# Score products on half the contraction rows and four heads each, in one score tile across two PSUM banks

## The chip, the cores and the metric

The kernel runs on one NeuronCore of a Trainium2 chip. The metric is the device time of one execution in microseconds (us); lower is better. Engines are named as in the profile: PE (TensorE, the matrix products; PEld is its weight load), DVE (VectorE), ACT (ScalarE), POOL (GpSimd) and SP (SyncE, which here issues the transfers).

## The reference, cut to what matters

The input x is 128 sequences of 32 tokens with 256 features. In the first layer each sequence is mixed along its 32 tokens by a 32 x 32 matrix that its subject picks, then goes through an attention whose four projections have quantised inputs and weights, and is added to x. A second mixing and a mixture of 16 experts (2 per token) follow. The change lies in the score products of the attention:

```
q, k, v = bitlinear(x, wq), bitlinear(x, wk), bitlinear(x, wv)   # each (128, 32, 256) -> 16 heads of 16
attn = einsum('bhqd,bhkd->bhqk', q, k) / sqrt(16)                # 16 heads, 32 x 32 scores per sequence
attn = where(causal, attn, -inf); attn = softmax(attn, -1)
out = einsum('bhqk,bhkd->bhqd', attn, v)
x = x + bitlinear(out, wp)
x = x + moe(mix(x))
```

## The kernel before

**Tiling.** The 4096 tokens are 32 tiles of 128 (`TILES`), four sequences each (`BT`), and a group is four tiles (`TG`, `GROUPS` = 8). Features live in two chunks of 128 (`KC` = 2), so a chunk holds 8 heads of 16 rows (`HC` = 8).

**The scores as block products.** Heads must not mix, though a product contracts over all its 128 rows. So the keys are spread out: `kx[g % 2]` has, for each chunk and each of its 8 heads, a copy of the transposed keys in which only the 16 rows of that head are filled, and the rest is zero for good (ACT clears `kx[0]` at L546, POOL clears `kx[1]` in `zero_kx1`, L464). `spread_k` (SP, L344) fills them with 8 transfers of 64 KB per group, once DVE has scaled the keys into `kT` (`scale_k`, L857). One product of `scores` (PE, L1180) then takes the 32 queries of one sequence as weights, 128 rows by 32 columns, and streams 8 heads times 32 keys, 256 columns; four sequences fill the four quarters of the output partitions. Two chunks and four sequences make 8 products of fp32 per tile, all on top of one product that lays down the causal mask (L1176, 512 columns, bf16). The result, 128 x 512, is one PSUM bank; tiles alternate between two banks, `ps_s[t % 2]`.

**What follows a score tile.** `copy_scores` (ACT, L636) copies the bank to `sc[t % 2]`, `row_max` (DVE, L867) takes the maximum per head, `sub_max` (POOL, L482) subtracts it, `exp_` (ACT, L647) takes the exponential, `transpose_p` (PE, L1193) and `copy_pT` (ACT, L658) turn it round, and `attend` (PE, L1208) multiplies by the values.

**The order of the work.** Each engine has one instruction stream, written out by hand in a function `iteration(it)` that is unrolled for `it` = 0 to 11. It works on several groups at once: mixing and projecting group `it`, scores and softmax of group `it - 1`, output projection of group `it - 2` (with its own quantisation: `centre_o` L573, `largest_o` L832, `factor_o` L838, `round_o` L582, `transpose_o` L1114, `project_o` L1219), second mixing, router (L1257) and ranks of group `it - 3`, and the scattering of rows to the experts' lists (POOL, L492) for group `it - 4`. Engines wait for each other by counting semaphores; a buffer is free when the count of its reader has come. For a score tile PE waits until ACT has copied the tile before the last (`sc_copied`).

After the loop 79 tiles of 128 rows pass the experts (L1335 to L1353 on PE), and the results are gathered and added up (L1059, L1061). This part uses the same memory (`arena`) for its weights, and starts to load them after the last score products that read it.

## Time and profile before

| | |
|---|---|
| median of 3 runs | 433.49 us (433.41 to 436.78) |
| profiled execution | 433.42 us, of it the span of the trace 431.6 us |
| PE busy | 324.8 us (75%) |
| DVE busy | 263.8 us (61%) |
| ACT busy | 248.7 us (58%) |
| POOL busy | 213.2 us (49%) |
| score products (L1180) | 35.8 us, in 512 records |
| mask products (L1176) | 12.6 us, in 32 records |

The span falls into a start of about 28 us, the loop over groups to about 252 us, the experts to about 400 us, and the gathering. Busy times are unions, so products that run side by side count once. A share of the whole span says little here: what an edit in the loop is worth is read from the loop.

### The profile page before, as it was taken

To read this page: it belongs to the slowest core of one execution; us is meant where nothing else is said; L and a number is where in the kernel's file an instruction comes from. 1 tells how busy PE (TensorE), PEld (TensorE's weight loads), DVE (VectorE), ACT (ScalarE), POOL (GpSimd) and SP (SyncE) were. 2 spreads that over 40 slices of the span, in tenths; PEclk is the share of its full clock that TensorE was granted. 3 is DMA by queue.
4 is the path that set the end of the run, shared out by engine and by line. 5 is a ranking of instruction groups with operands and counts; after the bars stand their busy time and mean duration, and the time that the engine had idled before them with its cause. 6 is when DMAs were issued, how large, how long until landed. Compare 5 with 4: busy or idle time off the path is not lost.

```text
span 431.6 us, 10950 instructions
## 1 busy us (share of the span) xinstructions
PE 324.8 (75%) x3257; PEld 249.9 (58%) x3257; DVE 263.8 (61%) x929; ACT 248.7 (58%) x580; POOL 213.2 (49%) x232
## 2 busy tenths in 40 slices
PE   0535989999999999999985800999799979993000
PEld 0332455767676676767574700898689868992000
DVE  2544477898888989898785373344344433441775
ACT  9144468787796978788676220566466645662000
POOL 3643123122473755647577854276657664664000
PEclk9968799999999999999997655899999999998555
DMA  6613555544546362534566695566646654631999
GB/s 232 173 53 68 137 114 114 116 102 82 124 134 161 99 182 66 159 85 119 145 186 185 165 293 205 141 180 170 176 133 179 177 159 120 183 100 32 379 400 357
DMA packets 76897, 68.87 MB, mean 160 GB/s; under 512 B 41003, under 2 KB 65968, under 8 KB 76721
## 3 DMA queue, kind: packets, MB, share of 16 engines
q1 hardware_dynamic: 65200, 44.03, 40.7%
q0 software_dynamic: 7296, 20.02, 12.7%
q10 hardware_dynamic: 4352, 4.20, 2.8%
q8 instruction: 28, 0.46, 0.5%
q14 instruction: 21, 0.16, 0.1%
HBM read 35.36 MB, written 30.62 MB: 153 GB/s over the span
## 4 chain that ended last, share of the span: by engine, by line
PE 46%; DVE 14%; issue 12%; DMA 6%; POOL 6%; SPq 6%; DVEq 5%; ACT 3%; POOLq 1%; ACTq 0%
PE bank L1342 9%; PE bank L1353 6%; PE bank L1180 5%; SPq L413 4%; POOL y_d L537 4%; DMA arena<-y_d 3%; PE bank L1335 3%; PE bank L1231 3%; PE bank L1257 3%; PE bank L1129 2%; SPq L344 2%; PE bank L1114 2%; PE bank L1208 2%; PE bank L1244 2%; PE bank L1193 2%
## 5 line engine op out<-in xcount | busy, mean ns | idle before, releaser
L537 POOL DMA_INDIRECT y_d<-cen,di x79 | 77.4, 980 | 53.2 <-issue 32.1
L1044 DVE SCALAR_TENSOR_TENSOR kT<-kT,hrow,bank 128x96 f32<-128x96 f32 x79 | 24.8, 314 | 78.4 <-ACT kT L732 77.6
L492 POOL DMA_INDIRECT routed<-hrow,posi x64 | 63.2, 987 | 17.0 <-issue 15.4
L1342 PE MATMUL bank<-arena,qT 128*128 x316 | 66.5, 334 | 0.0
L482 POOL TENSOR_TENSOR sc<-sc,mx 128x512 f32<-128x512 f32 x32 | 33.5, 1048 | 65.8 <-DVE mx L867 65.7
L1342 PEld LDWEIGHTS bank<-arena,qT 128*128 128x128 f32 x316 | 51.2, 196 | 0.2
L1335 PE MATMUL bank<-ident,hrow 128*128 128x128 f32 x158 | 31.7, 282 | 25.1 <-DMA hrow<-routed 19.0
L1353 PE MATMUL bank<-arena,sc 96*128 x158 | 48.0, 386 | 0.0
L737 ACT ACTIVATE cen<-bank 128x256 f32<-128x256 f32 x79 | 30.4, 384 | 25.0 <-PE bank L1353 24.0
L727 ACT ACTIVATE qT<-bank 128x256 f32<-128x256 f32 x79 | 29.9, 379 | 25.7 <-PE bank L1335 25.5
L1335 PEld LDWEIGHTS bank<-ident,hrow 128*128 128x128 f32 x158 | 22.5, 146 | 34.1 <-DMA hrow<-routed 19.7
L1180 PE MATMUL bank<-arena,qT 128*32 128x256 f32 x512 | 35.8, 399 | 0.0
L732 ACT ACTIVATE kT<-bank 128x96 f32<-128x96 f32 x79 | 19.9, 251 | 18.1 <-PE bank L1342 16.5
L658 ACT ACTIVATE pT<-bank 128x512 f32<-128x512 f32 x32 | 19.7, 614 | 12.2 <-PE bank L1193 11.8
L636 ACT ACTIVATE sc<-bank 128x512 f32<-128x512 f32 x32 | 19.6, 612 | 11.8 <-PE bank L1180 11.8
L1353 PEld LDWEIGHTS bank<-arena,sc 96*128 96x128 f32 x158 | 24.1, 192 | 3.6 <-issue 0.5
L867 DVE TENSOR_REDUCE mx<-sc 128x16 f32<-128x512 f32 x32 | 21.8, 680 | 4.9 <-ACT sc L636 4.9
L647 ACT ACTIVATE pr<-sc,s_qk 128x512 f32<-128x512 f32 x32 | 23.5, 735 | 2.0 <-POOL sc L482 1.8
L1208 PE MATMUL bank<-vx,pT 128*32 128x68 f32 x1024 | 21.8, 224 | 2.4 <-DVE cen L878 1.2
L1208 PEld LDWEIGHTS bank<-vx,pT 128*32 128x32 f32 x1024 | 16.8, 108 | 11.0 <-issue 6.6
L1180 PEld LDWEIGHTS bank<-arena,qT 128*32 128x32 f32 x512 | 13.7, 112 | 16.2 <-issue 11.0
L667 ACT ACTIVATE hrow<-bank 128x512 f32<-128x512 f32 x32 | 17.5, 603 | 9.2 <-PE bank L1231 7.7
(169 smaller groups left out, 732.1 us busy)
## 6 DMA issues: line engine op xcount, KB each, us to landing
hrow<-routed SPq DMA_DIRECT2D x79, 129.0 KB, 2.5
arena<-y_d SPq DMA_DIRECT2D x16, 512.0 KB, 12.3
v_d<-v_sb SPq DMA_DIRECT2D x8, 544.0 KB, 4.0
vx<-v_d SPq DMA_DIRECT2D x32, 136.0 KB, 3.5
X<-in_x SPq DMA_DIRECT2D x8, 512.0 KB, 3.7
arena<-kT SPq DMA_DIRECT2D x64, 64.0 KB
out_x<-X ACTq DMA_DIRECT2D x16, 256.0 KB, 8.7
arena<-in_L_ffn_gate_w SPq DMA_DIRECT2D x4, 384.0 KB, 3.6
```

Source lines behind the costliest of these rows:

```text
L482: g_.tensor_tensor(sc[t % 2][:, :, :], sc[t % 2][:, :, :], mx[t % 2][:, :].unsqueeze(2).to_broadcast([P, H, SEQ]), ALU.subtract).then_inc( ...
L492: g_.indirect_dma_start(routed, bass.IndirectOffsetOnAxis(ap=posi[g % 2][:, t, k:k + 1], axis=0), hrow[:, g % 2, t, k, :], None).then_inc( ...
L537: g_.indirect_dma_start(y_d, bass.IndirectOffsetOnAxis(ap=di[:, n:n + 1], axis=0), ye[n], None, bounds_check=Y_ROWS - 1, oob_is_err=False) ...
L647: a_.activation(pr[t % 2][:, :, :, :].rearrange("p c s j -> p s c j"), sc[t % 2][:, :, :].rearrange("p (s c) j -> p s c j", c=SLOTS), ACT. ...
L727: a_.activation(xeT[j % 2], bank[j % 2][:, 0:D].rearrange("p (c t) -> p c t", c=KC), ACT.Copy).then_inc(xeT_copied, 1)
L737: a_.activation(ye[n], bank[6 + n % 2][:, 0:D], ACT.Copy).then_inc(ye_copied, 1)
L1044: v.scalar_tensor_tensor(out=hh[n % 2], in0=sg[n % 2], scalar=xe[n][:, D + 1:D + 2], in1=bank[2 + n % 2][:, F:2 * F], op0=ALU.mult, op1=AL ...
L1180: last = t_.matmul(ps_s[t % 2][b * SEQ:(b + 1) * SEQ, c * HC * SEQ:(c + 1) * HC * SEQ], qT[g % 2][:, c, cols], kx[g % 2][:, c, :, cols], s ...
L1208: last = t_.matmul(o[b * SEQ:(b + 1) * SEQ, :, c, :], pT[t % 2][:, c, b * SEQ:(b + 1) * SEQ], vx[:, t * BT + b, :, c * VW:(c + 1) * VW], s ...
L1335: last = t_.transpose(bank[j % 2][:, c * P:(c + 1) * P], xe[j][:, c * P:(c + 1) * P], ident[:, :])
L1342: last = t_.matmul(bank[2 + n][:, 0:2 * F], xeT[n][:, c, :], gu[:, c, bass.ds(expert[m + LAG - 1], 1), :].rearrange("p o f -> p (o f)"), s ...
L1353: t_.matmul(bank[6 + n][:, 0:D], hhT[n], dw[:, bass.ds(expert[m], 1), :].rearrange("p o d -> p (o d)"), start=True, stop=True).then_inc(ye ...
```

## The change

It touches five places.

- The key buffers hold four heads per chunk side by side instead of eight (`HR` = 4): head h of a chunk lies in its 16 rows, at slot `h % 4`. Rows 0 to 63 of a slot so hold heads 0 to 3, and rows 64 to 127 heads 4 to 7. Each buffer is half as long, and so is its clear.
- A score product takes 64 rows (one half, `r`) instead of 128 and streams 4 heads, 128 columns, instead of 256. There are 16 per tile instead of 8, and the mask product becomes two of 256 columns.
- The two row halves write to two banks, `pair[:, 0]` and `pair[:, 1]`, each half filled. Both banks together are one tile; there is no second. So PE waits for the copy of the tile just before (`t` instead of `t - 1` in the count of `sc_copied`).
- The copy reads both half banks in one instruction and puts the heads back in their order in `sc`.
- In the order of the work, PE computes tile 2 after the two transposes of x instead of before them, and ACT copies tile 1 before `centre_o` and tile 2 before `copy_v(it, 0)`.

```diff
+HR = HC // 2
+HALF = KC * HR * SEQ
...
-    KX_WORDS = KC * HC * GT
-
-    kx = [arena[:, i * KX_WORDS:(i + 1) * KX_WORDS].rearrange("p (c h t) -> p c h t", c=KC, h=HC) for i in range(2)]
+    KX_WORDS = KC * HR * GT
+
+    kx = [arena[:, 2 * i * KX_WORDS:(2 * i + 1) * KX_WORDS].rearrange("p (c h t) -> p c h t", c=KC, h=HR) for i in range(2)]
...
-    bank = [ctx.enter_context(nc.psum_tensor(f"bank{i}", [P, 512], fp32)) for i in range(8)]
+    bank = [ctx.enter_context(nc.psum_tensor(f"bank{i}", [P, 512], fp32)) for i in range(3)]
+    pair = ctx.enter_context(nc.psum_tensor("pair", [P, 2, 512], fp32))
+    bank += [pair[:, 0, :], pair[:, 1, :]]
+    bank += [ctx.enter_context(nc.psum_tensor(f"bank{i}", [P, 512], fp32)) for i in range(5, 8)]
...
-                    sp.dma_start(kx[g % 2][rows, :, h, :], kT[rows, :, :]).then_inc(kx_in, 16)
+                    sp.dma_start(kx[g % 2][rows, :, h % HR, :], kT[rows, :, :]).then_inc(kx_in, 16)
...
-                a_.activation(sc[t % 2][:, :, :].rearrange("p h j -> p (h j)"), ps_s[t % 2][:, :], ACT.Copy).then_inc(sc_copied, 1)
+                a_.activation(sc[t % 2][:, :, :].rearrange("p (c r k) j -> p r c (k j)", c=KC, r=2),
+                              pair[:, :, 0:HALF].rearrange("p r (c n) -> p r c n", c=KC), ACT.Copy).then_inc(sc_copied, 1)
...
                 copy_scores(it - 1, 0)
+                copy_scores(it - 1, 1)
                 centre_o(it - 2)
-                copy_scores(it - 1, 1)
...
+                copy_scores(it - 1, 2)
                 copy_v(it, 0)
-                copy_scores(it - 1, 2)
...
-                if t >= 2:
-                    wait(pe, sc_copied, g, TG, t - 1)
+                if t >= 1:
+                    wait(pe, sc_copied, g, TG, t)
                 else:
-                    wait(pe, sc_copied, g, TG, TG + t - 1, lag=1)
-                t_.matmul(ps_s[t % 2][:, :], ident_b[:, :], causal_b[:, :].unsqueeze(1).to_broadcast([P, H, SEQ]), start=True, stop=False, skip_group_check=True)
+                    wait(pe, sc_copied, g, TG, TG, lag=1)
+                for r in range(2):
+                    t_.matmul(ps_s[r][:, 0:HALF], ident_b[:, :], causal_b[:, :].unsqueeze(1).to_broadcast([P, H // 2, SEQ]), start=True, stop=False, skip_group_check=True)
                 for c in range(KC):
                     for b in range(BT):
                         cols = slice(t * P + b * SEQ, t * P + (b + 1) * SEQ)
-                        last = t_.matmul(ps_s[t % 2][b * SEQ:(b + 1) * SEQ, c * HC * SEQ:(c + 1) * HC * SEQ], qT[g % 2][:, c, cols], kx[g % 2][:, c, :, cols],
-                                         start=False, stop=True, skip_group_check=True)
+                        for r in range(2):
+                            rows = slice(r * P // 2, (r + 1) * P // 2)
+                            last = t_.matmul(ps_s[r][b * SEQ:(b + 1) * SEQ, c * HR * SEQ:(c + 1) * HR * SEQ], qT[g % 2][rows, c, cols], kx[g % 2][rows, c, :, cols],
+                                             start=False, stop=True, skip_group_check=True)
...
                 mix2(it - 3, 1)
-                scores(it - 1, 2)
                 transpose_x(it, 0)
                 transpose_x(it, 1)
+                scores(it - 1, 2)
                 spread_s(it)
```

On PE, the stretch of a full turn from score tile 0 on stands so before (L1176 and L1180 are a score tile, L1257 the router, L1231 the second mixing, L1100 the transposes of x):

```order
L1176 MATMUL bank<-causal_b,ident_b 128x512 [waits sc_copied,q_copied,kx_in]
L1180 MATMUL bank<-arena,qT 32x256 x8
L1257 MATMUL bank<-rw,hT 128x16 [waits hT_copied,rw_in]
L1257 MATMUL bank<-rw,hT 128x16 x7
L1176 MATMUL bank<-causal_b,ident_b 128x512 [waits sc_copied]
L1180 MATMUL bank<-arena,qT 32x256 x8
L1231 MATMUL bank<-X,bd_0 128x256 [waits h_copied]
L1231 MATMUL bank<-X,bd_0 128x256
L1176 MATMUL bank<-causal_b,ident_b 128x512 [waits sc_copied]
L1180 MATMUL bank<-arena,qT 32x256 x8
L1100 MATMUL bank<-ident,cen 128x128 [waits z1_ok]
L1100 MATMUL bank<-ident,cen 128x128 x3
```

and after the change, from the router on, with L1183 and L1189 the score tile, L1266 the router, L1240 the mixing and L1106 the transposes:

```order
L1266 MATMUL bank<-rw,hT 128x16 [waits hT_copied,rw_in]
L1266 MATMUL bank<-rw,hT 128x16 x7
L1183 MATMUL pair<-causal_b,ident_b 128x256 [waits sc_copied]
L1183 MATMUL pair<-causal_b,ident_b 128x256
L1189 MATMUL pair<-arena,qT 32x128 x16
L1240 MATMUL bank<-X,bd_0 128x256 [waits h_copied]
L1240 MATMUL bank<-X,bd_0 128x256
L1106 MATMUL bank<-ident,cen 128x128 [waits z1_ok]
L1106 MATMUL bank<-ident,cen 128x128 x3
L1106 MATMUL bank<-ident,cen 128x128 [waits z1_ok]
L1106 MATMUL bank<-ident,cen 128x128 x3
L1183 MATMUL pair<-causal_b,ident_b 128x256 [waits sc_copied]
```

A tile is now two masks and 16 products on half as many columns, and tile 2 has moved behind the transposes.

On ACT, the stretch from the copy of tile 0 to that of V stands so before (L636 is the copy, L573 the centring of O, L667 the rows for the experts, L591 the copies of the transposes of x, L625 the copy of V):

```order
L636 ACTIVATE sc<-bank 128x512 [waits exp_ok,sc_ready]
L573 ACTIVATE cen<-cen,nmean 128x256 [waits o_var_ok]
L573 ACTIVATE cen<-cen,nmean 128x256 x3
L636 ACTIVATE sc<-bank 128x512 [waits exp_ok,sc_ready]
L667 ACTIVATE hrow<-bank 128x2x256 [waits h_ready]
L667 ACTIVATE hrow<-bank 128x2x256
L591 ACTIVATE xq<-bank 128x512 [waits v_ready,q_ready,xqT_ready] x2
L647 ACTIVATE pr<-sc,s_qk 128x4x4x32 [waits pT_ready,s1_ok,sub_ok]
L605 ACTIVATE s_row<-bank 128x512 [waits k_scaled,srow_ready]
L681 ACTIVATE ratio<-second 128x4 [waits second_ok]
L625 ACTIVATE v_sb<-bank,s_v 128x16x16 [waits v_put,s1_ok,v_ready]
L625 ACTIVATE v_sb<-bank,s_v 128x16x16
```

and after the change (L641, L578, L673, L596 and L630 in the same roles):

```order
L641 ACTIVATE sc<-pair 128x2x2x128 [waits exp_ok,sc_ready] x2
L578 ACTIVATE cen<-cen,nmean 128x256 [waits o_var_ok]
L578 ACTIVATE cen<-cen,nmean 128x256 x3
L673 ACTIVATE hrow<-bank 128x2x256 [waits h_ready]
L673 ACTIVATE hrow<-bank 128x2x256
L596 ACTIVATE xq<-bank 128x512 [waits v_ready,q_ready,xqT_ready] x2
L653 ACTIVATE pr<-sc,s_qk 128x4x4x32 [waits pT_ready,s1_ok,sub_ok]
L610 ACTIVATE s_row<-bank 128x512 [waits k_scaled,srow_ready]
L687 ACTIVATE ratio<-second 128x4 [waits second_ok]
L641 ACTIVATE sc<-pair 128x2x2x128 [waits exp_ok,sc_ready]
L630 ACTIVATE v_sb<-bank,s_v 128x16x16 [waits v_put,s1_ok,v_ready]
```

The copies of tiles 0 and 1 now stand together ahead of the centring, and that of tile 2 ahead of V.

## Rows read from the trace of the kernel before

**Rows 1.** Timeline of PE: start us, length us, operation, count [idle before <-releaser].

```profile
157.05 0.68 PE L1208 MATMUL bank<-vx,pT 128*32 128x68 f32 x32 [0.20 <-DVE cen L878]
...
181.45 0.68 PE L1208 MATMUL bank<-vx,pT 128*32 128x68 f32 x32 [0.21 <-DVE cen L878]
```

**Rows 2.** Busy us of PE, PEld, DVE, ACT, POOL in one turn; clock; DMA.

```profile
157.60:182.00 24.40, 24.09 (x327) 17.24 (x316) 21.96 (x79) 19.82 (x42) 14.14 (x14) 1.00 0.46 120
```

**Rows 3.** All waits of DVE from 84 to 206 us: total, times, longest.

```profile
DVE rs L876 <- PE bank L1208: 0.5, 1, 0.5
DVE amax L804 <- issue: 0.4, 1, 0.4
```

**Rows 4.** Timeline of DVE, then of POOL, in that turn.

```profile
162.49 1.14 DVE L825 TENSOR_SCALAR cen<-cen,mul 128x256 f32<-128x256 f32 x4
...
168.49 1.07 DVE L838 TENSOR_SCALAR amax<-amax 128x4 f32<-128x4 f32 x1
...
169.75 0.69 DVE L857 TENSOR_TENSOR kT<-bank,s_row 128x512 f32<-128x512 f32 x1
...
168.48 1.04 POOL L482 TENSOR_TENSOR sc<-sc,mx 128x512 f32<-128x512 f32 x1 [0.89 <-DVE mx L867]
```

**Rows 5.** Groups: shape, count | busy us, mean ns | idle before <-releaser.

```profile
L1180 PE MATMUL bank<-arena,qT 128*32 128x256 f32 x512 | 35.8, 399 | 0.0
...
L1208 PE MATMUL bank<-vx,pT 128*32 128x68 f32 x1024 | 21.8, 224 | 2.4 <-DVE cen L878 1.2 <-ACT pT L658 0.7
...
L636 ACT ACTIVATE sc<-bank 128x512 f32<-128x512 f32 x32 | 19.6, 612 | 11.8 <-PE bank L1180 11.8
...
L1176 PE MATMUL bank<-causal_b,ident_b 128*128 128x512 bf16 x32 | 12.6, 394 | 5.9 <-DMA arena<-kT 5.9
```

**Rows 6.** Timeline of PE, same turn: score tile 0, then the router.

```profile
158.94 1.07 PE L1180 MATMUL bank<-arena,qT 128*32 128x256 f32 x16
159.94 1.96 PE L1257 MATMUL bank<-rw,hT 128*128 128x16 f32 x16
```

**Rows 7.** Timeline of ACT, same turn: copy of tile 0, centring, copies of x.

```profile
160.13 0.63 ACT L636 ACTIVATE sc<-bank 128x512 f32<-128x512 f32 x1
160.60 1.74 ACT L573 ACTIVATE cen<-cen,nmean 128x256 f32<-128x256 f32 x4
...
166.03 1.08 ACT L591 ACTIVATE xq<-bank 128x512 bf16<-128x512 f32 x2 [0.72 <-PE bank L1100]
```

**Rows 8.** Timeline of PE: transposes of group 0, first mask and score tile.

```profile
28.48 1.97 PE L1100 MATMUL bank<-ident,cen 128*128 128x128 f32 x8 [7.01 <-DVE cen L825]
...
43.24 0.61 PE L1176 MATMUL bank<-causal_b,ident_b 128*128 128x512 bf16 x1 [4.37 <-DMA arena<-kT]
43.78 1.94 PE L1180 MATMUL bank<-arena,qT 128*32 128x256 f32 x16
```

**Rows 9.** Timeline of PE: transposes in the second turn with scores.

```profile
67.97 1.09 PE L1100 MATMUL bank<-ident,cen 128*128 128x128 f32 x8 [0.64 <-DVE cen L825]
```

**Rows 10.** Timelines of ACT and DVE, last turn with scores.

```profile
208.72 1.69 ACT L573 ACTIVATE cen<-cen,nmean 128x256 f32<-128x256 f32 x4
...
211.95 1.21 DVE L832 TENSOR_REDUCE amax<-cen 128x4 f32<-128x1024 f32 x1
...
213.85 1.06 DVE L838 TENSOR_SCALAR amax<-amax 128x4 f32<-128x4 f32 x1
```

**Rows 11.** Groups: the two clears of the key buffers.

```profile
L546 ACT ACTIVATE arena<-arena 128x8192 uint32<-128x8192 uint32 x1 | 7.0, 7030 | 0.0
L464 POOL MEMSET arena<- 128x8192 f32 x1 | 6.9, 6919 | 4.0 <-DVE cen L825 4.0
```

**Rows 12.** Busy us of the engines and granted clock in three stretches.

```profile
43.24:47.60 4.36, 4.36 (x34) 1.39 (x34) 3.09 (x11) 0.60 (x1) 0.42 (x1) 0.50 0.51 132
...
228.60:231.90 3.30, 1.28 (x12) 0.76 (x11) 2.98 (x17) 2.14 (x6) 2.49 (x4) 1.00 0.38 96
...
309.10:312.40 3.30, 0.13 (x1) 0.16 (x2) 0.38 (x3) 0.38 (x1) 1.78 (x2) 1.00 0.62 174
```

## The prediction

> **What bounds the kernel now.** I read the page first (it says PE 75%, DVE 61%, ACT 58% of the span), and then looked at where the changed work lies: the score products run only in the loop over groups, from 43 us on [rows 8]. What lies after that (routing, the 79 expert tiles, the last sums) keeps its instructions, so only the loop can move the time. The second view is the timeline of one full turn. Its first and last rows [rows 1] are the same 32 products, 24.40 us apart: this is the period of the loop, and before each of them PE has waited 0.2 us for a VectorE result. The busy time of that turn [rows 2] looks as if PE were the bound (24.09 of 24.40) and DVE had 2.4 us to spare (21.96). The third view corrects this. In the five turns from 84 to 206 us DVE waited for anybody just twice, 0.9 us in all [rows 3]. Its spare 2.4 us are the pauses of 0.07 to 0.10 us that its drains leave between small operations, some 28 in a turn: it is in its own order, back to back. A part of its turn is neither work nor a wait that a view names: an operation on 4 columns (L838) stands with 1.07 us, just as long as POOL's subtraction beside it [rows 4]; DVE released that subtraction itself, with the row maximum before it. So **two engines are full**, DVE with nothing spare and PE with 0.2 us. Time taken from PE alone buys nothing in a full turn.
>
> **The products.** Each fp32 product stands in the trace as two records: 16 for the 8 products of a score tile (rows 5 count 512 for 32 tiles), 32 for the 16 of the attention. The 16 records of a score tile take 1.07 us with the tail of the last, 1.00 until PE goes on [rows 6]; their mean of 399 ns each, 16 in 1.07 us, shows several running at once, on the four output quarters. After the change it has 32 records on half the columns. Bounds: if the two row halves run side by side, half the columns give 0.50; if they don't, it stays 1.00. The row nearest to the new shape is L1208, also 32 records, of 68 columns and 32 output rows: 21.8/32 = 0.68 us per tile, 21 ns per record [rows 5]. I take 0.62 us, between 0.50 and 0.68: **0.38 us saved per tile**, 1.5 per full turn. Far out stands the case that each record keeps its 62 ns: 2.0 us. The Trainium skill (TensorE: Matmul & The Clock Gate, section Back-to-back issue gap) has a floor of about 25 ns from start to start however few columns there are. By that floor 32 records take 0.80 us and a tile saves 0.20. The trace does not agree (21 ns in L1208), so the row decides.
>
> The mask product becomes two of 256 columns instead of one of 512 (12.6/32 = 0.39 with its tail, 0.22 before the next starts): same columns, one more weight load, which overlaps. I charge 0 to 0.1 us and take 0.05.
>
> **The single tile.** Scores of tile t now wait for the copy of tile t-1 instead of t-2. The copy is 0.61 us [rows 5], and with the handing over on both sides it is 0.7 from the last product to the next. In a full turn, in the clock times of rows 6 and 7:
> - Tile 0 to 1: the router stands between, 1.9 us [rows 6]. Tile 0 ends at 159.6, its copy cannot start before ACT is free (160.13 [rows 7]), and is over at 160.8; the router ends at 161.5. Wait 0.
> - Tile 1 to 2: mix2 and the transposes stand between. These wait for DVE (L825 ends at 163.63 [rows 4]), as PE comes to them at 163.4 (tile 1 to 162.35, mix2 1.06): wait 0.2. Tile 2 then stands behind the transposes, while ACT copies them out (1.1 us [rows 7]), time in which PE did the spreading of the scales before.
> - Tile 2 to 3: its copy was moved ahead of the V copy on ACT, and lands at 168.4; PE arrives at 168.1. Wait 0.3.
> - On ACT, the centring of O (L573, 1.74 us) is queued behind copy 1, so behind tile 1: it ends at 164.5 instead of 162.3. DVE comes to it 1.9 us before its L838, that is at 166.6 (the maximum over O, 1.21, and a row maximum, 0.68, lie between), so it costs nothing here.
> - After tile 3 PE needs DVE's scaled keys (L857, 170.44 [rows 4]); it was there at 170.5 before and is there early now, and waits.
>
> So PE saves 1.5, gives 0.5 back in new waits and idles for the rest. What DVE takes from PE and ACT (the four copies, router scores, ranks, projections) arrives 0.2 us or more earlier or at the time before. **Full turns: 0.** No transfer changes its size; the key DMAs are released by DVE's L857, thus at the same times.
>
> **The first turns.** Scores of group 0 start at 43.24, when the keys land, at half clock: 1.9 us a tile [rows 8]. Tile 0 and 1 save 0.9 each, the copy between them costs 0.7, the transposes come 1.1 earlier and so partly into half clock, which costs 0.5, and tiles 2 and 3 save 0.7. With 0.2 lost in meeting ACT, this is **1.1 less**. In the next turn PE was idle before the transposes, with tile 2 done [rows 9]. Now tile 2 stands behind them, on the path: +0.9, of which tile 3 gives back 0.38 and ACT's queue hides 0.1: **+0.4**.
>
> **The last turn with scores** (207 us on) has no transposes of x and DVE is not full. There the centring counts: it ran at 208.72, while ACT waited for tile 1 [rows 10]. Now: tile 0 ends at 207.75, router to 209.65, tile 1 to 210.6, copy to 211.2, centring (1.7) to 212.9. DVE's L832 started on it at 211.95 and now can at 212.9; L838 behind it (again beside POOL) gives ACT its factors 0.9 later, and the transposes of O, project_o and the residual follow. **+0.9.** If DVE's other operations (den, pos) took its place, it would be +0.5.
>
> **Zeroing** kx halves from 7.0 (ACT) and 6.9 us (POOL) [rows 11]. ACT's is its first work, long before DVE's first moments let it go on; POOL's starts with the end of DVE's first L825, at 28.4, and only the second group's keys need it, a turn later. Nothing waits for either: 0. If DVE was slowed by it, it would be a gain of some tenths.
>
> **The clock.** PE's gaps grow from 0.64 to 1.9 us in the second turn with scores, and one of 0.7 is put into the first burst, which ran without a gap at half clock (1.2 GHz) for 4.4 us before 2.4 GHz was granted [rows 12]. Around 228.6 a stretch with 1.28 us busy of 3.30 was followed by half clock, yet a pause of 3.2 us among the expert tiles was not [rows 12]. So a lost stretch is possible at three places (43, 66 and 212 us). The eight transposes take 1.97 us at half clock [rows 8] and 1.09 at full [rows 9], so what PE has to do there, some 1.6 us of it on the path each time, costs as much again: 0 to 1.6 us per place. I take 0.8 for the three together.
>
> **Sum:** -1.1 + 0.4 + 0 + 0.9 + 0.8 = +1.0, against the profiled execution of 433.42 us (span 431.6), which stands 0.07 below the median of the runs, 433.49. Forecast **434.4 us**.
>
> **Rivals.**
> 1. **The row halves don't overlap** (they do leave through separate banks, but nothing in this trace shows two row halves at once). Then PE keeps its 24.1 us of work and gets 0.5 us of waits and 0.2 of masks: 24.8 to 25.0 per turn instead of 24.4. PE becomes the bound: 0.5 over six turns (the five full ones and the one before) is +3.0, and the first turns lose their gain (+1.1): 438.5. It decides as soon as a tile takes over 0.9 us. For it: no row here. Chance 0.10.
> 2. **The copy becomes the bound.** If ACT is late at each tile, PE stands 0.7 us four times, 2.8 against 1.5 saved. A turn is 24.1 + 1.3 = 25.4, six turns +6.0: 440. It decides once ACT begins a copy later than the work between two tiles lasts. Against it: the router and the transposes between the tiles [rows 6]. Chance 0.05. The Trainium skill (TensorEngine Tiling (Array Packing), section PSUM Bottleneck) points this way: tiling speeds up the products but not their way out of PSUM.
> 3. **PE was the bound** and DVE only looks full, because its pauses and the 1.07 us rows stretch. Then 1.5 - 0.5 = 1.0 per turn comes back, six turns -6, the ends +0.2: 428. Against it: rows 3 and the 0.2 us that PE waits for DVE each turn. Chance 0.07.
> 4. **Records keep their pace** of 62 ns: 1.0 more per tile, over 20 us slower. Chance 0.03.
>
> The forecast has the remaining 0.75. It includes up to three clock stretches (to 438) and none of them (433.6), and the ends of the ramps (431.9 if the last turn costs nothing and the clock holds). The **range** is 431.6 to 438.6: it leaves out rivals 2, 3 and 4 and little else. A change of 1%, 4.3 us, is about what a measurement of this kernel can tell from none. Faster by more: rival 3, 0.07. Slower by more: rivals 1, 2 and 4, 0.18. Within: 0.75.
>
> **What would show it.** In the changed profile: the group of score products at 0.6 us per tile with 32 records; PE's idle time before the transposes and before tile 3's mask, released by DVE and by the ACT copy; the period between two turns still 24.4, with DVE's list of waits as short as before; DVE's L832 of the last turn late; the granted clock at 44 to 50, 66 to 72 and 212 to 218. The prediction is wrong if the period of the full turns moves by over 0.3 us either way, or if DVE in them waits for PE or ACT.

## The result, and the profile after

| | before | after |
|---|---|---|
| median | 433.86 us (432.02 to 436.78, 20 runs) | 436.55 us (434.97 to 440.12, 20 runs) |
| ratio after/before | | 1.0064, 95% interval 1.0045 to 1.0083 |
| profiled execution (span) | 433.42 (431.6) | 437.44 (435.7) |

The changed kernel is 2.7 us slower, 0.6%. Another series, that of e4 below, gave 438.00 against 434.47 (ratio 1.0085, 1.0053 to 1.0118). Ratios leave out executions over 1.5% above the fastest of their kernel: one of twelve in e2 and in e3, and five of twelve in e6, its profiled one among them. The length of the changed kernel's profile and the busy times of its page:

```profile
span 435.7 us, 12023 instructions
...
PE 313.3 (72%) x3786; PEld 254.0 (58%) x3801; DVE 263.7 (61%) x929; ACT 244.5 (56%) x580; POOL 209.6 (48%) x232
```

PE has 11.5 us less to do, DVE what it had, ACT and POOL 4.2 and 3.6 less (most of it the halved clears), and the kernel is slower. The groups that answer to [rows 5] and [rows 11] (shape, count | busy, mean ns | idle before):

```profile
L1189 PE MATMUL pair<-arena,qT 64*32 64x128 f32 x1024 | 22.2, 284 | 0.0
L641 ACT ACTIVATE sc<-pair 128x512 f32<-128x512 f32 x32 | 19.5, 608 | 17.0 <-PE pair L1189 17.0
L1183 PE MATMUL pair<-causal_b,ident_b 128*128 128x256 bf16 x64 | 12.9, 284 | 7.2 <-DMA arena<-kT 5.7 <-ACT sc L641 1.5
L551 ACT ACTIVATE arena<-arena 128x4096 uint32<-128x4096 uint32 x1 | 3.6, 3616 | 0.0
L469 POOL MEMSET arena<- 128x4096 f32 x1 | 3.5, 3507 | 4.0 <-DVE cen L831 4.0
```

The product group fell from 35.8 to 22.2 us, the two clears halved, the masks and copies stand as they were. Now the full turn of [rows 1], [rows 2], [rows 4] and [rows 6], first PE's timeline (start, length, operation, count [idle before <-releaser]):

```profile
157.81 0.68 PE L1217 MATMUL bank<-vx,pT 128*32 128x68 f32 x32 [0.21 <-DVE cen L884]
...
159.38 0.38 PE L1183 MATMUL pair<-causal_b,ident_b 128*128 128x256 bf16 x2
159.69 0.67 PE L1189 MATMUL pair<-arena,qT 64*32 64x128 f32 x32
160.29 1.96 PE L1266 MATMUL bank<-rw,hT 128*128 128x16 f32 x16
...
164.44 1.09 PE L1106 MATMUL bank<-ident,cen 128*128 128x128 f32 x8 [0.31 <-DVE cen L831]
...
171.58 0.38 PE L1135 MATMUL bank<-xq,wT 128*128 128x512 bf16 x1 [1.01 <-DVE kT L863]
...
182.22 0.68 PE L1217 MATMUL bank<-vx,pT 128*32 128x68 f32 x32 [0.21 <-DVE cen L884]
```

A score tile lasts 0.60 us until PE goes on (159.69 to 160.29). No wait for the copy L641 stands in the turn; PE waits for DVE instead, 1.01 us at the scaled keys, and the period is 24.41. That turn in the view of busy time (length, then busy us of PE, PEld, DVE, ACT, POOL, granted clock, DMA share, GB/s), and all waits of DVE from 84 to 206 us:

```profile
157.60:182.00 24.40, 22.59 (x382) 17.48 (x384) 21.96 (x78) 19.69 (x42) 14.13 (x14) 1.00 0.45 116
```

```profile
DVE mv L791 <- issue: 0.5, 1, 0.5
DVE amax L810 <- issue: 0.4, 1, 0.4
```

PE gave up 1.50 us of the turn, DVE's 21.96 us are those of [rows 2], and its waits sum to the same 0.9 us as in [rows 3]. So the full turns are as forecast, and the time was lost elsewhere. The four turns between the first masks of groups 2 to 6 last 24.36, 24.45, 24.76, 24.40 before and 24.35, 24.47, 24.76, 24.42 after.

**The ends of the loop.** The second turn with scores, PE:

```profile
63.35 0.39 PE L1183 MATMUL pair<-causal_b,ident_b 128*128 128x256 bf16 x2 [1.04 <-DMA arena<-kT]
63.67 0.67 PE L1189 MATMUL pair<-arena,qT 64*32 64x128 f32 x32
65.10 0.39 PE L1183 MATMUL pair<-causal_b,ident_b 128*128 128x256 bf16 x2 [0.76 <-ACT sc L641]
...
68.00 1.09 PE L1106 MATMUL bank<-ident,cen 128*128 128x128 f32 x8 [1.91 <-DVE cen L831]
68.92 0.38 PE L1183 MATMUL pair<-causal_b,ident_b 128*128 128x256 bf16 x2
69.24 0.67 PE L1189 MATMUL pair<-arena,qT 64*32 64x128 f32 x32
69.83 1.16 PE L1130 MATMUL bank<-ident,step_of 128*128 128x128 f32 x8
```

The transposes come when DVE lets them, at 68.00 as at 67.97 in [rows 9]; PE's idle time before them grew from 0.64 to 1.91 us, and tile 2 stands behind them. The turn lasts 22.45 us instead of 21.76. The last turn with scores, DVE, ACT and PE, for [rows 10]:

```profile
211.27 1.69 ACT L578 ACTIVATE cen<-cen,nmean 128x256 f32<-128x256 f32 x4
...
213.00 1.22 DVE L838 TENSOR_REDUCE amax<-cen 128x4 f32<-128x1024 f32 x1 [1.16 <-ACT cen L578]
...
214.90 1.06 DVE L844 TENSOR_SCALAR amax<-amax 128x4 f32<-128x4 f32 x1
...
219.85 1.05 PE L1228 MATMUL bank<-wT,oq 128*128 128x256 bf16 x8 [0.30 <-ACT oq L603]
```

DVE now waits 1.16 us for O's centring. Counted from the first mask of the last group (206.76 before, 206.97 after), project_o starts 12.88 us later instead of 12.11.

**This pair of profiles does not show the loss.** On the clock of the execution project_o was 0.97 us late (219.85 against 218.88), yet the experts began at the same time. The last half of the last group's second mixing ran at half clock in the profile before and at full clock in the one after, and that alone gave 0.94 us back. Before, then after:

```profile
245.99 2.05 PE L1231 MATMUL bank<-X,bd 128*128 128x256 f32 x4
...
268.74 1.51 PE L1335 MATMUL bank<-ident,hrow 128*128 128x128 f32 x4 [19.03 <-DMA hrow<-routed]
```

```profile
246.97 1.11 PE L1240 MATMUL bank<-X,bd 128*128 128x256 f32 x4
...
268.73 1.33 PE L1344 MATMUL bank<-ident,hrow 128*128 128x128 f32 x4 [19.03 <-DMA hrow<-routed]
```

The 4.1 us between the two spans lie behind that, 2.0 in the experts and 2.1 in what follows them, where no instruction changed and where profiles of one kernel differ by as much. The loss shows in the medians; what it is made of has to be read from the turns of many profiles.

### The profile page after: what moved, and what is told of

Its sections match the earlier page's. It is cut to its first block, busy times and chain, and to the rows that moved or that the text cites. A ratio compares the mean times of both kernels' runs of the same rounds, so it can differ in the third digit from the quotient of the medians.

```text
span 435.7 us, 12023 instructions
## 1 busy us (share of the span) xinstructions
PE 313.3 (72%) x3786; PEld 254.0 (58%) x3801; DVE 263.7 (61%) x929; ACT 244.5 (56%) x580; POOL 209.6 (48%) x232
## 4 chain that ended last, share of the span: by engine, by line
PE 37%; DVE 22%; issue 13%; DVEq 7%; POOL 6%; DMA 6%; SPq 5%; ACT 3%; POOLq 1%; ACTq 0%
PE bank L1362 6%; PE pair L1351 5%; PE bank L1351 5%; SPq L418 4%; POOL y_d L542 4%; PE bank L1344 3%; DMA arena<-y_d 3%; DVE stats L891 2%; PE bank L1120 2%; DVE X L901 2%; PE bank L1253 2%; DVE cen L884 2%; DVE stats L785 2%; PE bank L1228 2%; PE bank L1135 2%
## 5 line engine op out<-in xcount | busy, mean ns | idle before, releaser
L487 POOL TENSOR_TENSOR sc<-sc,mx 128x512 f32<-128x512 f32 x32 | 33.5, 1047 | 66.7 <-DVE mx L873 66.6
L1050 DVE SCALAR_TENSOR_TENSOR kT<-kT,hrow,bank 128x96 f32<-128x96 f32 x40 | 12.6, 315 | 39.9 <-ACT kT L738 39.1
L1050 DVE SCALAR_TENSOR_TENSOR kT<-kT,hrow,pair 128x96 f32<-128x96 f32 x39 | 12.3, 314 | 40.4 <-ACT kT L738 40.4
L1351 PE MATMUL bank<-arena,qT 128*128 x160 | 34.0, 337 | 0.0
L1351 PE MATMUL pair<-arena,qT 128*128 x156 | 33.8, 342 | 0.0
L641 ACT ACTIVATE sc<-pair 128x512 f32<-128x512 f32 x32 | 19.5, 608 | 17.0 <-PE pair L1189 17.0
L1351 PEld LDWEIGHTS bank<-arena,qT 128*128 128x128 f32 x160 | 26.3, 198 | 0.4 <-issue 0.3
L1351 PEld LDWEIGHTS pair<-arena,qT 128*128 128x128 f32 x156 | 26.1, 201 | 0.0
L569 ACT ACTIVATE cen<-bank,nmean 128x256 f32<-128x256 f32 x32 | 12.5, 475 | 19.7 <-DVE veps L794 19.7
L475 POOL TENSOR_TENSOR rstd<-veps,half 128x4 f32<-128x4 f32 x8 | 8.2, 1029 | 31.8 <-DVE veps L794 31.8
```

Source lines behind the costliest of these rows:

```text
L487: g_.tensor_tensor(sc[t % 2][:, :, :], sc[t % 2][:, :, :], mx[t % 2][:, :].unsqueeze(2).to_broadcast([P, H, SEQ]), ALU.subtract).then_inc( ...
L1050: v.scalar_tensor_tensor(out=hh[n % 2], in0=sg[n % 2], scalar=xe[n][:, D + 1:D + 2], in1=bank[2 + n % 2][:, F:2 * F], op0=ALU.mult, op1=AL ...
L1351: last = t_.matmul(bank[2 + n][:, 0:2 * F], xeT[n][:, c, :], gu[:, c, bass.ds(expert[m + LAG - 1], 1), :].rearrange("p o f -> p (o f)"), s ...
```

## The experiments

They ran in three series, each on a chip of its own and each against the kernel before on that chip: e1 to e4, e5 to e8, and e9 to e11. Only the first of the three has the changed kernel in it (e4), so across series ratios are compared and not times. Theories: A, the new order costs time at the loop's ends. B, the single score tile makes PE or ACT wait in every turn. C, later stages shift by chance. D, shorter products leave gaps in which TensorE's granted clock stays at or falls to 1.2 GHz.

**e1, old order on half rows.** Single tile and half rows stay; PE and ACT get their old order (B, or the shape alone, against A).

```diff
-                transpose_x(it, 0)
-                transpose_x(it, 1)
                 scores(it - 1, 2)
+                transpose_x(it, 0)
+                transpose_x(it, 1)
...
                 copy_scores(it - 1, 0)
-                copy_scores(it - 1, 1)
                 centre_o(it - 2)
+                copy_scores(it - 1, 1)
...
-                copy_scores(it - 1, 2)
                 copy_v(it, 0)
+                copy_scores(it - 1, 2)
```

> The changed kernel with the order of before: PE computes tile 2 ahead of the transposes of x, ACT centres O between the copies of tiles 0 and 1 and copies V before tile 2. The half-row products and the single tile stay. Theory A (the loss comes from the new order: tile 2 behind the transposes in the second turn with scores, +0.4 to +0.7, and the centring behind tile 1 in the last, +0.3 to +0.9): 1 to 1.6 us faster than the changed kernel, so a ratio to before of about 1.001 or less, and in its profile the centring of O in the last turn starts right behind the copy of tile 0. Theory B (the loss comes from the single tile, whose wait the order was meant to hide): slower than the changed kernel, 438 or more, with full turns over 24.4 us. Theory C (the loss lies outside the loop, in the clock of the later stages): no difference beyond 0.5 us.

Measured: 436.73 us, ratio 1.0053 (1.0024 to 1.0082). Full turns 24.19 to 24.76 us, so the single tile costs nothing there and B falls for the full turns. In the first turn, where tile 2 now stands right behind tile 1, it does cost time: PE waits 0.76 us for the copy ahead of tile 1 and again ahead of tile 2, and the turn takes 20.89 us instead of 19.70. The last group's project_o came 11.68 us after its first mask, so the order is what had cost time there. Yet theory A's ratio of 1.001 or less did not come: the second turn with scores lasted 24.05 us, with the clock fallen. That started theory D.

**e2, new order alone.** The kernel before (full rows, two tiles) in the new order.

```diff
-                scores(it - 1, 2)
                 transpose_x(it, 0)
                 transpose_x(it, 1)
+                scores(it - 1, 2)
...
                 copy_scores(it - 1, 0)
-                centre_o(it - 2)
                 copy_scores(it - 1, 1)
+                centre_o(it - 2)
...
-                copy_v(it, 0)
                 copy_scores(it - 1, 2)
+                copy_v(it, 0)
```

> The kernel before with the new order alone (PE's tile 2 behind the transposes, ACT's copies of tiles 1 and 2 earlier); full-row products, two tiles. Theory A: the order costs its 1 to 1.5 us here too, and more where PE is full: PE has only 0.2 us to spare per turn, and tile 2 now stands in front of the spreading of the scales, so up to 0.3 us per turn: ratio to before 1.003 to 1.007. Theory B: no difference. Theory C: no difference, or one as large as in the changed kernel if it comes from the order through the clock.

Measured: 437.82 us, ratio 1.0072 (1.0035 to 1.0109). The order alone makes this kernel as slow, as theory A forecast (up to 1.007), and without the clock: its mean time at half clock is 94.9 us per execution, where the kernel before has 92.7 in that series. Second turn 23.02 us (at 2.4 GHz throughout), project_o of the last turn 13.63 us after the first mask, 1.5 later than before: full tiles make the centring wait longer than half ones.

**e3, PE's old order only.** The changed kernel; ACT keeps the new order.

```diff
-                transpose_x(it, 0)
-                transpose_x(it, 1)
                 scores(it - 1, 2)
+                transpose_x(it, 0)
+                transpose_x(it, 1)
```

> The changed kernel with only PE's order put back (tile 2 ahead of the transposes); ACT keeps the new order. Theory A: the second turn with scores gets its 0.4 to 0.9 us back, the last turn does not: 0.5 to 0.9 faster than the changed kernel and slower than with both put back by 0.3 to 0.9. Theory B: PE waits for the copy of tile 1 before tile 2 in every turn, 0.2 to 0.7 us, hidden or not; if not hidden, full turns of 24.6 to 25.1. Theory C: no difference.

Measured: 438.61 us, ratio 1.0085 (1.0054 to 1.0116), level with the changed kernel (e4) and not 0.5 to 0.9 faster as theory A had it. The last turn is as in the changed kernel (12.87), so that loss comes with ACT's order and not PE's. The first turn with scores is 21.66 us, 2 more than in the changed kernel; the second 23.67, with the clock down in it.

**e4, the changed kernel again**, word for word, as control in the same series.

> The changed kernel once more, word for word, for a second profile and its time against before on this chip. Ratio 1.0045 to 1.0083 as measured. Theory A and B: the loop from the landing of the first keys to the last score tile takes the same as in its first profile, within 0.3 us. Theory C: the later stages (experts, gathering) differ from profile to profile by 1 to 3 us with the position of the half-clock stretches, and the mean of them is what the change costs.

Measured: 438.00 us, ratio 1.0085. Its profile differs from the first one of the same kernel in one place, the second turn with scores, PE:

```profile
64.33 0.67 PE L1189 MATMUL pair<-arena,qT 64*32 64x128 f32 x32
67.83 1.97 PE L1106 MATMUL bank<-ident,cen 128*128 128x128 f32 x8 [2.83 <-DVE cen L831]
69.59 0.63 PE L1183 MATMUL pair<-causal_b,ident_b 128*128 128x256 bf16 x2
70.15 1.05 PE L1189 MATMUL pair<-arena,qT 64*32 64x128 f32 x32
```

After 2.83 us without work the eight transposes take 1.97 us instead of 1.09 and the tile 1.05 instead of 0.67: the clock is at half. This turn took 24.84 us instead of 22.45, 0.9 of it from the first mask to the transposes, and 1.5 behind them. The 0.9 began a turn earlier: the first burst of the scores ran at half clock for 7.9 us instead of 6.0, and DVE released the transposes 25.15 us after the first mask of all instead of 24.35.

**e5, the gaps of the second turn filled.** Products without a use, from the identity and the projection weights, into a bank that is free then.

```diff
+            def fill(n, ps):
+                for _ in range(n):
+                    t_.matmul(ps[:, :], ident_b[:, :], wT[:, 0, :, :].rearrange("p c o -> p (c o)"), start=True, stop=True)
...
+                if it == 2:
+                    fill(4, ps_c)
                 scores(it - 1, 0)
                 router(it - 3)
+                if it == 2:
+                    fill(3, ps_c)
                 scores(it - 1, 1)
                 mix2(it - 3, 1)
+                if it == 2:
+                    fill(8, ps_c)
```

> The changed kernel with 15 additional products on TensorE (identity by 512 columns of the projection weights, 0.21 us each at 2.4 GHz, into the router's bank, which nothing uses yet), all in the second turn with scores: 4 ahead of the first score tile (TensorE idles 1.04 us there), 3 ahead of the second (0.76), 8 ahead of the transposes of x (1.91). They leave the result alone and keep TensorE at work where it otherwise waits. Theory D (clock): the changed kernel's shorter products leave gaps in this turn, and in many executions the granted clock falls to 1.2 GHz there; that turn lasted 22.45 us where it stayed and 24.84 where it fell. With the gaps filled the clock stays in every execution: second turn 22.3 to 22.6 us in the profile, mean time per execution at half clock about 97 us instead of 102 to 107, median lower by 1 to 1.5 us, ratio to the kernel before about 1.005. Theory A (order of the work alone): a turn's length does not hang on what fills TensorE's waits; nothing changes, ratio 1.0085 as in the control run of the changed kernel.

Measured: 436.34 us, ratio 1.0037 (1.0010 to 1.0063). The kernel does more work and its ratio is lower than the changed kernel's in either series, though the intervals overlap. PE in that turn:

```profile
66.19 0.67 PE L1189 MATMUL pair<-arena,qT 64*32 64x128 f32 x32
66.80 1.90 PE L1287 MATMUL bank<-wT,ident_b 128*128 128x512 bf16 x8
68.87 1.09 PE L1106 MATMUL bank<-ident,cen 128*128 128x128 f32 x8 [0.17 <-DVE cen L831]
```

The turn is 22.55 us, the transposes run at full clock. The mean time per execution at half clock (worked out as twice the missing part of the mean granted clock times the span) was 95.7 us, against 106.6 in e4 and 102.3 in the first series of the changed kernel.

**e6, O's centring put back in the last turn alone.**

```diff
                 copy_scores(it - 1, 0)
+                if it == GROUPS:
+                    centre_o(it - 2)
                 copy_scores(it - 1, 1)
-                centre_o(it - 2)
+                if it != GROUPS:
+                    centre_o(it - 2)
```

> The changed kernel, where in the last turn with scores alone (it == GROUPS) ScalarE centres O between the copies of tiles 0 and 1, as before the change, and in every other turn behind the copy of tile 1. Theory A (order): the last turn loses the 1.0 us that O's maximum came late (14.. the turn from first mask to last mask of the last group 8.3 to 7.3 us), everything behind it follows 1.0 us earlier, median 1.0 us under that of the changed kernel, ratio to the kernel before 1.0085 - 0.0023 = about 1.006. Theory D (clock alone): the 1.0 us comes back at the last turn but the stage of the experts takes it up, since TensorE's clock there depends on when the pause begins; ratio 1.0085.

Measured: 435.58 us over all 12 executions against 434.12, that is 1.0034; the ratio 0.9998 (0.9960 to 1.0035) rests on seven of them, so I build on neither. The trace of the last turn shows what the edit did there, DVE:

```profile
214.33 1.21 DVE L841 TENSOR_REDUCE amax<-cen 128x4 f32<-128x1024 f32 x1
216.22 1.07 DVE L847 TENSOR_SCALAR amax<-amax 128x4 f32<-128x4 f32 x1
```

Its first mask is at 209.54, so the maximum starts 4.79 us later; in the changed kernel it was 6.03 (213.00 - 206.97). Project_o follows at 11.63 instead of 12.88. This profile had half clock in the second turn again, which took 25.83 us.

**e7, every loss mended.** e6, tile 2 ahead of the transposes in the second turn, and products without a use in three places.

```diff
+                if it == 1:
+                    fill(8, ps_c)
+                if it == 2:
+                    fill(4, ps_c)
                 scores(it - 1, 0)
                 router(it - 3)
+                if it == 2:
+                    fill(3, ps_c)
                 scores(it - 1, 1)
                 mix2(it - 3, 1)
+                if it == 2:
+                    fill(3, ps_c)
+                if it == 2:
+                    scores(it - 1, 2)
+                    fill(3, ps_c)
                 transpose_x(it, 0)
                 transpose_x(it, 1)
-                scores(it - 1, 2)
+                if it != 2:
+                    scores(it - 1, 2)
...
                 iteration(it)
+            fill(70, ps_c)
```

> The changed kernel with the place of each loss mended: ScalarE's old order in the last turn, TensorE's old place of tile 2 (ahead of the transposes of x) in the second turn with scores, and additional products without a use (8 ahead of the first score tile of all, 13 in the second turn with scores, 70 between the last ranking and the experts, where TensorE waits 19 us for the routed rows). Theory D with A: first turn 19.6 (new order) or less, second turn 22 or less without half clock, last turn 7.3, the stage of the experts begins at full clock and is 2 to 3 us shorter; median 431 to 433, ratio 0.992 to 0.998. If only the order counts: ratio 1.004, that is 436. If the additional products stand in the way of the work (they can't be overtaken), it is above the changed kernel's 1.0085.

Measured: 433.30 us, ratio 0.9974 (0.9946 to 1.0001). The loss is gone. The stage of the experts was not 2 to 3 us shorter: 125.86 us, where the kernel before has 125.75 to 128.91 (below).

**e8, the kernel before, filled.** Full rows, two tiles, old order, products without a use alone.

```diff
+                if it == 1:
+                    fill(8, ps_c)
+                if it == 2:
+                    fill(4, ps_c)
                 scores(it - 1, 0)
...
                 scores(it - 1, 2)
+                if it == 2:
+                    fill(3, ps_c)
...
+            fill(70, ps_c)
```

> The kernel before, with full rows, two score tiles and its own order, and additional products without a use: 8 ahead of the first score tile, 4 ahead of the second turn's first, 3 behind its third, 70 ahead of the experts. It tells what the two ways of making the score products are worth where the clock is the same in both. Theory D: both gain by the filled pause ahead of the experts; this one has 0.4 us more of score products in each tile, which costs nothing where VectorE sets the turn (24.4 us), and so it ends within 1 us of the kernel with half rows and filled gaps: median 431 to 433, ratio 0.993 to 0.998. Rival (score products on half the rows are worth something once the clock is out of the way): this one ends 1 to 3 us behind the other.

Measured: 432.47 us, ratio 0.9978 (0.9946 to 1.0010). e7 and e8 can't be told apart, nor either from no gain over the kernel before. With the losses at the ends mended, half rows are worth nothing that shows.

**e9, both causes mended, nothing else.** e5 and e6 together.

```diff
+                if it == 2:
+                    fill(4, ps_c)
...
+                if it == 2:
+                    fill(3, ps_c)
...
+                if it == 2:
+                    fill(8, ps_c)
...
+                if it == GROUPS:
+                    centre_o(it - 2)
                 copy_scores(it - 1, 1)
-                centre_o(it - 2)
+                if it != GROUPS:
+                    centre_o(it - 2)
```

> The changed kernel with the 15 additional products in the second turn with scores and, in the last turn alone, ScalarE's centring of O back between the copies of tiles 0 and 1. If the two causes add up (theory A for the last turn, 1.0 us; theory D for the second turn, 1.3 to 1.8 us), the last group's masks span 7.3 us, the second turn lasts 22.3 to 22.6 without half clock, and the kernel is level with the one before: ratio 0.999 to 1.003. If one of them only hid the other, it stays at the 1.0037 that the additional products alone gave.

Measured: 434.01 us against 434.18, ratio 0.9991 (0.9960 to 1.0022), at 95.1 us of half clock per execution. With both mended the kernel is level with the one before, and the interval lies clear below both of the changed kernel's (1.0045 to 1.0083, 1.0053 to 1.0118). Alone, e5 gave 1.0037 and e6 1.0034 over all its executions, so the two add up as far as the intervals tell; how the loss divides between them is not measured, as the intervals of the single ones overlap the changed kernel's. One forecast missed: in the profile the last group's masks span 8.71 us and not 7.3, because the clock fell there, at 210.3 us, although PE had been idle for at most 0.45 us at a time in the eight us before:

```profile
207.00:214.00 7.00, 6.56 (x98) 4.63 (x106) 5.10 (x25) 4.17 (x9) 3.08 (x3) 0.76 0.63 151
```

The 0.76 before the DMA share is the mean granted clock. So the third of the prediction's places, the last turn, can lose the clock as well; no other profile shows it there. Project_o came at 12.78 us, so in this one execution the mended order gained almost nothing.

**e10 and e11, the kernel before again**, word for word, for two more profiles of it.

> The kernel before, word for word, for a second profile of it. Theory D: in the second turn with scores TensorE keeps 2.4 GHz (no half clock between 61 and 80 us), as in the three profiles of kernels with full rows so far, the turn lasts 21.6 to 21.9 us; in four of the five profiles with half rows and unfilled gaps it fell. If that is chance of the single execution, it shows half clock there about as often as the changed kernel: the turn is then 23.5 to 25.8 us.

> The kernel before, word for word, for a third profile of it. As for the second: theory D says 21.6 to 21.9 us and no half clock in the second turn with scores; chance says half clock there about as often as in the changed kernel, and 23.5 us or more.

Measured: 438.68 and 436.04 us, one execution each. Neither has half clock in the second turn; e10's turn of 22.18 us is 0.3 above the forecast, as its transposes waited 1.04 us for DVE. The second turn with scores in busy time and clock, e10, then e11, then e4:

```profile
63.56:85.74 22.18, 20.91 (x289) 14.67 (x289) 17.35 (x54) 17.47 (x38) 6.12 (x7) 1.00 0.52 120
```

```profile
63.52:85.20 21.68, 20.90 (x288) 14.66 (x289) 16.95 (x53) 16.95 (x37) 5.92 (x6) 1.00 0.54 123
```

```profile
62.26:87.10 24.84, 20.84 (x354) 15.86 (x357) 17.66 (x56) 18.16 (x40) 6.58 (x7) 0.93 0.49 110
```

All thirteen profiles, for the places that matter, in us. "To the transposes" is from the second turn's first mask to its transposes of x, "then" from there to the first mask of the turn after, "first burst" from the first mask of all to the rise of the clock, "project_o" from the last group's first mask to the next project_o:

| profile | second turn | to the transposes | then | half clock in it | first burst | project_o |
|---|---|---|---|---|---|---|
| before | 21.76 | 4.68 | 17.09 | none | 4.4 | 12.11 |
| e10, e11 | 22.18, 21.68 | 5.08, 4.61 | 17.09, 17.08 | none | 4.7, 4.6 | 12.11, 12.12 |
| e8, full rows, filled | 21.67 | 4.63 | 17.04 | none | 4.7 | 12.11 |
| e2, full rows, new order | 23.02 | 4.76 | 18.26 | none | 3.5 | 13.63 |
| after | 22.45 | 4.64 | 17.80 | none | 6.0 | 12.88 |
| e4, after again | 24.84 | 5.57 | 19.28 | 3.4 | 7.9 | 12.88 |
| e1, half rows, old order | 24.05 | 5.85 | 18.20 | 3.4 | 7.9 | 11.68 |
| e3, half rows, PE old | 23.67 | 5.73 | 17.95 | 6.8 | 9.3 | 12.87 |
| e6, half rows | 25.83 | 5.59 | 20.24 | 6.8 | 6.2 | 11.63 |
| e5, e9, half rows, filled | 22.55, 22.68 | 4.74, 4.88 | 17.80, 17.80 | none | 7.9, 6.4 | 12.89, 12.78 |
| e7, half rows, filled, tile 2 back | 22.08 | 5.08 | 17.00 | none | 6.8 | 11.63 |

The column "then" takes the second turn apart: 17.0 to 17.1 with tile 2 ahead of the transposes at full clock, 17.80 with half tiles in the new order, 19.28 and 20.24 where the clock fell as well. So the order is 0.7 us (1.2 with full tiles, e2) and a fall of the clock 1.5 to 2.4. In e1 and e3 the clock fell before the transposes, so its cost there is spread over both columns.

With half rows and open gaps the clock fell in four of five profiles, with full rows in none of five, and with half rows and filled gaps in none of three. The traces do not tell which gap does it, and the length of one gap does not decide. In e4 and e6 the clock fell within the gap ahead of the transposes (2.83 and 2.85 us long), in e6 1.7 us after its start; yet the first profile of the changed kernel kept it through a gap of 1.91 us there, and e2 through 2.04. In e1 and e3 PE has no gap ahead of the transposes, and it came to them late because the clock had fallen already, at 68.7 and 66.6 us, in a gap of 1.53 us and in one of 0.76.

After the start of the scores the clock also comes up later with half rows, and that costs time too. From the first mask of all to the second turn's transposes, which DVE releases, it took 24.35, 24.47 and 24.52 us where the first burst lasted 6.0 to 6.4 us (after, e6, e9), 25.15 and 25.19 where it lasted 7.9 (e4, e5), and 24.73 to 24.89 in the three profiles of the kernel before. The first 8 us from the first mask, after and e11:

```profile
43.65:51.65 8.00, 7.24 (x121) 5.02 (x122) 3.43 (x12) 3.04 (x6) 2.09 (x2) 0.63 0.52 109
```

```profile
43.28:51.28 8.00, 8.00 (x68) 3.82 (x69) 3.81 (x12) 2.44 (x5) 2.09 (x2) 0.71 0.56 127
```

With full rows PE was busy all 8.00 us and had the clock at a mean of 0.71; with half rows it was busy 7.24 and had 0.63, and in e4, busy 7.24 as well, 0.51.

## Why the prediction was right, and what in it was not

- **Two engines are full, so a full turn gains nothing: held.** PE gave up 1.50 us per turn and the period moved by 0.02 at most. Rival 3 (PE was the bound) is out.
- **The products, 0.62 us a tile: 0.60.** The row halves run side by side; rivals 1 and 4 are out. Of the two ways to price it, the row of the attention's 32 records held and the 25 ns floor of the Trainium skill (TensorE: Matmul & The Clock Gate, Back-to-back issue gap) did not, if each of the two records of a product is counted as a start: 32 records in 0.60 us are 19 ns each.
- **Masks +0.05: nothing.** 0.31 us from the mask to the products after (159.38 to 159.69), no more than before.
- **Single tile, waits 0 / 0.2 / 0.3: 0 / 0.31 / 0**, and the 0.31 is DVE's and not the copy's; all hidden, so rival 2 is out. PE waits 1.01 us for DVE's scaled keys instead, as it was said to.
- **Zeroing 0: held**, with the clears at 3.6 and 3.5 us and the first mask at 43.65 and 42.68 in two profiles against 43.24, 43.75 and 43.28.
- **First turn with scores, -1.1: -0.4 at best.** 19.70 and 19.58 us against 20.06, 19.81 and 20.24 from mask to mask. What counts is the way on to the second turn's transposes: 0.4 us shorter than before where the first burst lasted 6.0 us (24.35 against 24.73 to 24.89), and 0.3 longer where it lasted 7.9 (25.15). I had saved the products' time at half clock and charged 0.7 for the waits, but let the clock rise when it did before; it rose 1.3 to 3.5 us later.
- **Second turn, +0.4: +0.7 where the clock held** (17.80 against 17.09 from the transposes on). Spreading and projections came 0.9 to 1.0 later, as worked out (69.83 against 68.91); less of it was given back.
- **Last turn, +0.9: +0.77** at project_o, and +0.85 at the ranking of the group before the last. e3 and e6 show that ACT's order does it: it costs 1.25 us within the changed kernel (12.88 against 11.63), and the shorter tiles give 0.5 back (11.63 against 12.11).
- **The clock, 0.8 for three places: too small. This is the term that was mis-sized.** The other terms, as measured, come to -0.4 + 0.7 + 0.8 = +1.1. The medians lie 2.7 us apart in one series and 3.5 in the other, so 1.6 to 2.4 are left for it. The clock levels carry that much: the mean time at half clock rose from about 93 us per execution to 102 and 107, and over the 213 executions of all kernels, each with a level of its own, a microsecond more of it went with 0.23 us (0.20 to 0.26) more time, which makes 2.1 to 3.1. That is a correlation, and not all such time costs something: e8 had only 72 us of it and was at most 1.7 us faster. The test is e5, where work was only added, in that one turn: the half clock went back to 96 us and the ratio down to 1.0037, within reach of the changed kernel's intervals, and with e6's order it went to 0.9991 in e9, clear of them. Read place by place, the longer first burst cost 0.7 to 0.8 us (25.15 against 24.35 and 24.47), a fall in the second turn 1.5 or 2.4, and the one in the last turn of e9 1.5 (masks over 8.71 us instead of 7.24 in e6). The bound of 1.6 us per place, from eight transposes at both levels, was about right but for the longer fall.

The sum said +1.0 and it was +2.7: the right mechanisms, with the clock's term too small. The range held the time. Two of its figures were badly worked out: with nothing lost in the last turn and the clock held, the terms give 432.7 and not 431.9, and rival 1, priced at 438.5, lies inside the range that it is counted out of. Nor does it take 1% to tell a change from none: twenty executions of each kernel showed 0.6%. [Rows 12] had shown that a stretch with gaps could be followed by half clock, yet I took 0.8 us for three places, as if each had a chance of about one in six; four of the five profiles with half rows and open gaps had it in the second turn alone.

What stays open: which idle time makes the clock fall, and when; how often it falls in the third place, the last turn (one profile in thirteen); and why the stage of the experts varies. From the first expert product to the last store issued the experts took 125.75, 128.76 and 128.91 us in the three profiles of the kernel before, 127.73 and 128.67 in two of the changed one, with no instruction changed. The profile on which the prediction rested was the shortest of the three. What follows the last store issued took 37.1 to 37.4 us in most profiles, and 39.2 to 39.3 in the first of the changed kernel and in e10. e7 and e8 filled the pause ahead of the experts and had 125.86 and 127.03, which is within what the kernel before does by itself. No run filled the second turn of the kernel before and nothing else, so what the added products are worth there without half rows is not measured.

## What to carry to other kernels

Time taken from an engine that already waits for another one turns into gaps, and where such an engine is TensorE, the gaps can have a price of their own: the granted clock. Before making its products shorter, look at the ends of the loop, where there is little other work to fill in, and price a lost clock there by the rows at both levels. When an edit reorders an in-order queue to suit the full turns, cost it apart in the first and last turn, where the neighbours that hid the wait are absent: here one moved centring cost 1.25 us in the last turn with half tiles, 1.5 with full ones, and nothing in the full turns. And compare a stage between two kernels only with the spread of that stage within one kernel beside it.

## What the runs showed of the hardware

- Two products on separate row halves of the array, into separate PSUM banks, ran side by side: 32 records of 128 columns in 0.60 us, where 16 of 256 columns took 1.00. The same at half clock: 1.11 us with the tail in place of 1.94.
- One kernel, two executions: an idle stretch of PE of 1.91 us was followed by full clock, one of 2.83 us at the same place by half clock. But the length of a gap alone does not tell: in e3 the clock fell when no idle stretch of the ten us before had been over 1.16 us, in e9 while PE worked and had been idle for at most 0.45 us at a time in the eight us before, and e2 kept it through 2.04 us. One profile does not tell whether a kernel keeps its clock; the mean over the executions does.
- Of the kernel before, three executions' experts differ by 3.2 us with the same instructions, which is more than the 2.7 us between the medians of one series and nearly the 3.5 of the other.
- Time at half clock is not all alike. 70 products without a use in the 19 us pause ahead of the experts (15.27 us long in e7) helped to bring it down from 93 to 79 us (e7) and 72 (e8) per execution, and the time moved by 0.8 and 1.7 us. In the profile before, some 27 us at half clock lay around that pause (245.7 to 272.9), 19 of them while PE waited for the routed rows.
